# Seven of sixteen heads turned by DMA instead of by TensorE in the first stage of a two-layer gated attention and expert kernel

## The reference, cut to what matters

```python
q = _split_heads(hidden_states_query @ Wq.T + bq)
k = _split_heads(hidden_states_key @ Wk.T + bk)
v = _split_heads(hidden_states_key @ Wv.T + bv)
scale = 1.0 / np.sqrt(HEAD_DIM)
scores = jnp.einsum('bhqd,bhkd->bhqk', q * scale, k)
scores = scores + ((1.0 - attention_mask) * -10000.0)[:, None, :, :]
probs = jax.nn.softmax(scores, axis=-1)
ctx = jnp.einsum('bhqk,bhkd->bhqd', probs, v)
```

## Time and profile before

| | us |
|---|---|
| median of 3 runs | 1444.75 (1437.92 to 1447.92) |
| the profiled execution | 1443.42 |
| its span in the profile | 1441.8 |
| PE busy | 1264.8 (88%) |
| DVE busy | 1092.9 (76%) |
| ACT busy | 1003.9 (70%) |
| POOL busy | 827.7 (57%) |

### The profile page before, as it was taken

How to read it: one execution, slowest core, us unless ns; L and a number is a source line. 1 busy time by engine, 2 the same in 40 slices (tenths; PEclk the granted TensorE clock), 3 DMA queues, 4 the chain that set the end, 5 groups by cost and what they waited for, 6 DMA issues and landing times. The chain is left out here.

```text
span 1441.8 us, 44028 instructions
## 1 busy us (share of the span) xinstructions
PE 1264.8 (88%) x13508; PEld 916.7 (64%) x13508; DVE 1092.9 (76%) x3110; ACT 1003.9 (70%) x2584; POOL 827.7 (57%) x1204
## 2 busy tenths in 40 slices
PE   5999999999985599999998999999999985389994
PEld 3788888888864245656665556656566653278993
DVE  4899999999984268887887877878788873367772
ACT  3988788887883368787776777777787872155662
POOL 3645444454455445777676776777677675045663
PEclk9999999999997699999999999999999996599997
DMA  6233343333400148877666766767576784753323
GB/s 172 86 120 112 106 121 98 118 99 121 120 24 17 48 92 160 159 137 148 136 148 136 151 137 140 141 145 156 122 146 138 146 186 85 285 173 60 61 35 74
DMA packets 303968, 175.19 MB, mean 122 GB/s; under 512 B 250234, under 2 KB 291586, under 8 KB 300720
## 3 DMA queue, kind: packets, MB, share of 16 engines
q1 hardware_dynamic: 287632, 130.94, 40.8%
q0 software_dynamic: 13168, 35.80, 9.8%
q10 hardware_dynamic: 3024, 6.47, 1.6%
HBM read 64.48 MB, written 41.96 MB: 74 GB/s over the span
## 5 line engine op out<-in xcount | busy, mean ns | idle before, releaser
L1663 ACT ACTIVATE b_prob<-b_prob,b_top 112x487 f32<-112x487 f32 x256 | 178.9, 699 | 42.8 <-DVE b_top L1789 40.9
L1296 POOL TENSOR_TENSOR b_halves<-b_prob,b_halves 112x487 f16<-112x487 f32 x128 | 152.3, 1190 | 88.4 <-ACT b_halves L1688 86.6
L1474 PE MATMUL b_ps_p<-w_s,b_tok_s 128*128 128x512 f16 (+1 forms) x768 | 187.7, 381 | 5.6 <-DVE b_k_s L1776 5.3
L1474 PE MATMUL b_ps_p<-b_tok_s,w_s 128*128 128x487 f16 x768 | 188.0, 384 | 4.7 <-POOL b_tok_s L1290 3.7
L1789 DVE CUSTOM_DVE_ANT_0 b_prob<-b_ps_s,b_keep 112x487 f32<-112x487 f32 x256 | 167.7, 656 | 32.1 <-PE b_ps_s L1567 31.8
L701 ACT ACTIVATE a_prob<-a_prob,a_top 112x375 f32<-112x375 f32 x256 | 156.4, 611 | 4.5 <-DVE a_top L837 3.4
L1688 ACT ACTIVATE b_halves<-b_prob 112x487 f16<-112x487 f32 x256 | 156.0, 609 | 0.4
L837 DVE CUSTOM_DVE_ANT_0 a_prob<-a_ps_s,a_keep 112x375 f32<-112x375 f32 x256 | 138.6, 541 | 21.8 <-PE a_ps_s L593 19.2
L1582 PEld LDWEIGHTS b_ps_o<-b_v_s,b_pT 128*128 128x128 f16 (+1 forms) x3072 | 124.9, 100 | 32.7 <-DMA b_pT<-b_halves 11.0
L1582 PE MATMUL b_ps_o<-b_v_s,b_pT 128*128 128x64 f16 (+1 forms) x3072 | 136.1, 195 | 9.0 <-DMA b_pT<-b_halves 8.9
L842 DVE TENSOR_TENSOR a_pT<-a_ps_t,a_pT 125x336 f16<-125x336 f32 x256 | 128.6, 503 | 18.4 <-ACT a_pT L708 12.4
(11 more groups left out here) (262 smaller groups left out, 3063.0 us busy)
## 6 DMA issues: line engine op xcount, KB each, us to landing
xs<-a_blank SPq DMA_DIRECT2D x14, 1032.0 KB, 4.0
c_w_pool<-w_split SPq DMA_DIRECT2D x8, 1600.0 KB, 10.9
b_wch_f<-in_w_experts POOLq DMA_DIRECT2D x32, 384.0 KB, 4.9
w_split<-b_wch_s POOLq DMA_DIRECT2D x32, 384.0 KB, 4.0
a_ctx_f<-in_ctxT SPq DMA_DIRECT2D x16, 375.0 KB, 3.9
a_k_stack<-a_k_s SPq DMA_DIRECT2D x64, 93.8 KB, 2.8
b_ctx_t<-in_ctx SPq DMA_DIRECT2D x16, 375.0 KB
c_xt<-xs SPq DMA_DIRECT2D x35, 129.0 KB, 2.5
```

The lines of the kernel that those rows point to most:

```text
L1296: pool.tensor_tensor(halves[:, h % TURN, LO, 0:NK], prob[:, h % RING, 0:NK], halves[:, h % TURN, HI, 0:NK], ALU.subtract).then_inc(s_lo[1], 1)
L1474: last = pe.matmul(out, sta(a, k), mov(m, k), start=(k == 0 and n == 0), stop=(k == tiles - 1 and n == 2))
L1663: act.activation(prob[:, h % RING, 0:NK], prob[:, h % RING, 0:NK], ACT.Exp, bias=top[:, h % RING:h % RING + 1], scale=-1.0, accum_out=sums ...
```

## The change

Of the 16 heads of each batch of the first stage, seven (`BY_DMA`: 1, 3, 5, 7, 9, 11, 13) no longer go through PE's transposes. ACT copies their exponentials to f16 rows (`high_half`, in slot h+1), POOL makes the low rows (`low_half`, slot h+2), and SP turns both by one transposing DMA (`turn`, slot h+3). Their value products stand six slots behind their scores, those of the nine others (`BY_PE`) four, as before; slot 5 has none and slot 3 of the next batch has two. The nine share one bank `ps_t` (before two). The freed bank holds the second half of the values: heads 0 to 7 are in one bank, 8 to 15 in the other, read out in slots 15 and 4 (of the next batch). Blocks of keys are 128, 128 and 119 (before 3 x 125). `v_s` has a column of ones behind the 32 value columns, so the value product gives the row sums too, and the exponentials are taken without accumulator.

The lists of POOL and SP, before one item after the other, are now given by slot, with the low halves and the turns between the other items. `load_residual` is issued a batch earlier, the store a batch later. `pT` grows from four to eight heads, and POOL sets five more regions at the start, which the other engines wait for. The semaphores of the turns are made once for both stages, so the second stage counts on from what the first has sent.

```diff
-        pT = sb("pT", [128, RING, 2, NB0, 128], F16)
+        TURN = 8
+        prob = sb("prob", [T, RING, CP], F32)
+        halves = sb("halves", [T, TURN // 2, 2, CP], F16)
+        pT = sb("pT", [128, TURN, 2, NA, 128], F16)
...
+        BY_DMA = tuple(range(1, H - 2, 2))
+        BY_PE = tuple(h for h in range(H) if h not in BY_DMA)
+        VSLOT = {s: [s - 4] if s % 2 == 0 else [s - 6] for s in range(4, H + 4)}
+        VSLOT[5] = []
+        VSLOT[H + 3] = [H - 3, H - 1]
@@ SyncE @@
+            def turn(b, h):
+                need_all(sp, settled, (s_lo, len(BY_DMA), b, BY_DMA.index(h) + 1), valued(b, h - TURN))
+                sp.dma_start(pT[:, h % TURN, :, :, 0:T].rearrange("p s j n -> p (s j) n"),
+                             halves[:, h // 2 % (TURN // 2), :, :].rearrange("p s n -> p (s n)"),
+                             transpose=True).then_inc(s_turned[h // 2 % (TURN // 2)], 16)
             def body(b, par):
+                for s in range(H):
+                    if s == 1 and ahead(b, 1):
+                        load_mask(b + 1, 1 - par)
+                    if s == 2 and not early(b, 2):
+                        store(b - 2)
+                    if s == 3 and ahead(b, 2):
+                        load_tokens(b + 2)
+                    if s == 5 and ahead(b, 1):
+                        stack_keys(b + 1, 1 - par)
+                    if s == 9 and ahead(b, 1):
+                        mask_queries(b + 1, 1 - par)
+                    if s == 11:
+                        clear_rows(b)
+                    if s == 13:
+                        load_residual(b)
+                    c, _, h = heads(s, 3, b, par)
+                    if h in BY_DMA and not (first(b) and s < 3):
+                        turn(c, h)
...
 @@ GpSimd @@
             def body(b, par):
+                for s in range(H):
+                    if s == 0 and not first(b):
+                        residual_bias(b - 1)
+                    if s == 1 and ahead(b, 1):
+                        deviation_x(b + 1)
+                    if s == 2 and ahead(b, 1):
+                        mask_bias(b + 1, 1 - par)
+                    if s == 4 and not first(b):
+                        residual(b - 1)
+                    if s - 2 in BY_DMA:
+                        low_half(b, s - 2)
+                    if s == 5 and not first(b):
+                        deviation_x1(b - 1)
+                    if s == 6 and ahead(b, 1):
+                        split_queries(b + 1)
+                    if s == 8 and ahead(b, 2):
+                        context_high(b + 2)
+                    if s == 10 and ahead(b, 2):
+                        context_low(b + 2)
+                    if s >= 12 and not first(b):
+                        add_expert(b - 1, s - 12, ahead(b, 2))
+                    if s >= 8 and first(b):
+                        experts_low(s - 8)
...
             def exps(b, h):              # ACT
+                act.activation(prob[:, h % RING, 0:C], prob[:, h % RING, 0:C], ACT.Exp, bias=top[:, h % RING:h % RING + 1],
+                               scale=-1.0).then_inc(s_exp, 1)
+            def high_half(b, h):
+                act.activation(halves[:, h // 2 % (TURN // 2), HI, 0:C], prob[:, h % RING, 0:C], ACT.Copy).then_inc(s_hi, 1)
@@ TensorE @@
             def values(b, par, h):
+                if h in BY_DMA:
+                    need(pe, *turned(b, h))
+                        last = pe.matmul(ps_o[h // 8][:, col:col + VW - 1], pT[0:r, h % TURN, part, j, :],
+                                         v_s[par][0:r, j, h, 0:VW - 1], start=(h % 8 == 0 and j == 0 and part == HI),
+                                         stop=(j == NA - 1 and part == LO), skip_group_check=True)
@@ VectorE @@
+            def read_out(c, i):
+                dve.reciprocal(rsum[:, group], out[:, :, 2 * D0]).then_inc(s_rsum, 1)
+                dve.tensor_tensor(o_f[:, group, :], out[:, :, 0:D0], o_lo[:, group, :], ALU.add).then_inc(s_oread, 1)
```

More of the change, by code:

```diff
@@ L385, in _ @@
             mask_queries(0, 0)
-            sp.wait_ge(s_blank, 1)
+            sp.wait_ge(s_zero, 2)
             run_batches(sp, body)
+            turn(B - 1, H - 3)
+            store(B - 2)
             store(B - 1)
@@ L455, in next_low, with add_expert, finish @@
                 pool.tensor_tensor(next_w[:, LO, cols], next_f[:, cols], next_w[:, HI, cols], ALU.subtract).then_inc(s_nlo, 1)
[L457 to L465, removed]
+            def add_expert(c, j, alone=True):
+                if not alone:
+                    for n in range(2):
+                        next_low((c - (B - 3)) * 8 + 2 * j + n)
+                need(pool, s_scaled, E // 2, c, j + 1)
+                need(pool, s_odd if j else s_x2, E // 2 if j else 1, c, j)
+                pool.tensor_tensor(acc_odd[:, :], scaled[j % 2][:, :], (acc_odd if j else x1)[:, :], ALU.add).then_inc(s_odd, 1)
+            def finish(c):
                 need(pool, s_odd, E // 2, c, E // 2)
@@ L471, in body @@
             def body(b, par):
-                if ahead(b, 1):
-                    deviation_x(b + 1)
-                if not first(b):
-                    residual(b - 1)
-                    deviation_x1(b - 1)
-                if ahead(b, 1):
-                    mask_bias(b + 1, 1 - par)
-                    split_queries(b + 1)
-                if ahead(b, 2):
-                    split_context(b + 2)
-                if not first(b):
-                    sum_experts(b - 1, ahead(b, 2))
-                if first(b):
-                    for n in range(H // 2):
-                        experts_low(n)
-            split_context(0)
+                for s in range(H):
[21 more added lines that the diff above has]
+                        experts_low(s - 8)
+                if not first(b):
+                    finish(b - 1)
+            context_high(0)
+            context_low(0)
             mask_bias(0, 0)
@@ L619, in values @@
                 last.then_inc(s_pv, 1)
-            def drain(b, par):
-                for s in range(4):
-                    for lag, stage in ((2, transposes), (4, values)):
-                        h = H + s - lag
-                        if h < H:
-                            stage(b, h) if lag == 2 else stage(b, par, h)
             def body(b, par):
@@ L630, in body @@
                     scores(b, par, s)
-                    if not (first(b) and s < 2):
-                        c, _, h = heads(s, 2, b, par)
+                    c, _, h = heads(s, 2, b, par)
+                    if h in BY_PE and not (first(b) and s < 2):
                         transposes(c, h)
-                    if s == 5:
-                        values(b, par, 0)
-                    if s != 4 and not (first(b) and s < 4):
-                        values(*heads(s, 4, b, par))
+                    for h in VSLOT.get(s + H, []):
+                        if not first(b):
+                            values(b - 1, 1 - par, h)
+                    for h in VSLOT.get(s, []):
+                        values(b, par, h)
                     if ahead(b, 1):
@@ L651, in _ @@
             run_batches(pe, body)
-            drain(B - 1, 1)
+            for s in range(H, H + 4):
+                if s - 2 < H:
+                    transposes(B - 1, s - 2)
+                for h in VSLOT[s]:
+                    values(B - 1, 1, h)
             for k in range(DI):
@@ L1114, in phase_attention_large_heads @@
         s_lo = [sem("lo_even"), sem("lo_odd")]
-        s_turned = [sem(f"turned{i}") for i in range(RING)]
         s_pv = sem("pv")
@@ L2273, in build_program @@
         s_rows = ctx.enter_context(nc.semaphore("rows"))
+        s_turned = [ctx.enter_context(nc.semaphore(f"turned{i}")) for i in range(4)]
         with nc.sbuf_tensor("w1_s", [128, 2, WKV + WQ + WOUT], F16) as w1_s:
```

205 lines of the change are left out of this document (120 added, 85 removed).

## The result

The changed kernel takes **1552.88 us** as the median of 4 runs (1550.92 to 1557.06), the kernel before 1446.34 in the same comparison. The ratio is **1.0744**, with a 95% interval of 1.0682 to 1.0806. The direction of the forecast was right, the size was not: 1468 was forecast, 1484 was the top of the range. All runs in this document are in the chip's fast state but one of e10's six, which is left out of its time and ratio.

The account below looks back on a forecast made before the run. PE was taken to set the first stage's pace, DVE close behind. Fourteen batches x 1.1 (15.4), clock 7 and ends 2 gave +24.4 on 1443.4 us: 1468 us, range 1434 to 1484 (without rival outcomes 1454 to 1484).

Parts of the forecast that it names:

- The chain through POOL and SP: First stage: head 7's turn waits on SP behind `mask_queries`, is issued at 13.2 and lands 16.3 us after the read-out.
- When does PE want it?: First stage, slot 13: PE is ready for head 7's values 13.1 us after the read-out.
- the 3 us stall: First stage, slot 13: PE stands about 3 us at head 7's values in each batch that prepares a next one.
- the total of PE's waits for turned heads in the stage: Sign of the forecast: PE's values wait for transposed `a_pT`, 35 to 45 us in total, always behind eight mask transfers.
- The rest of the loop, 10.6 us: First stage, from head 7's values to the next read-out: 11.06 us before, 10.6 after, making the period 26.9 us.
- Rival 3: First stage: POOL's two-input low parts hold up DVE's two normalisations by up to 0.9 us each, 1493 us; chance 0.05.
- The clock: 0.5 us a batch: First stage: half clock behind PE's 3 us stall costs 0 to 1.2 us a batch, taken as 0.5, 7 us over 14 batches.
- The other stages only get other semaphore counts: nothing: Outside the first stage: only semaphore counts change, so no time is added.
- The ends of the stage: First stage, batches 0, 14, 15 and drain: late POOL low parts against a missing stall and a shorter normalisation, sum +2 us.
- The capacity argument: First stage: if only capacity counted, the 25.8 us period would fall to 23.6, or about 23.9 with the second read-out.

Follow-up runs that it names:

- e10: e7 with POOL's low part of head 9 waiting until the gate weights are written: 1463.8 us, ratio 1.0132.
- e4: e1 with `clear_rows` (1 MB to DRAM) moved on SP from slot 11 to slot 15: 1480.5 us, ratio 1.0210.
- e3: e1 with POOL's `context_low` moved from slot 10 to the end of slot 14: 1501.2 us, ratio 1.0356.
- e11: e10 with POOL adding the expert's part ahead of two next-stage low parts in the last two batches: 1455.9 us, ratio 1.0093.
- e1: The changed kernel with 16 more small DVE instructions ahead of its first-stage loop: 1506.6 us, ratio 1.0382.
- e7: e6 with `clear_rows` at slot 1, POOL's `mask_bias` at slot 4 and 40 small ACT instructions ahead of the loop: 1460.1 us, ratio 1.0073.
- e9: e7 without the 16 DVE instructions ahead of the loop, their tile kept: 1515.9 us, ratio 1.0497.
- e6: e1 with `context_low` at slot 14, `clear_rows` at slot 15 and `mask_queries` in halves at slots 9 and 11: 1482.1 us, ratio 1.0199.
- e5: e1 with `mask_queries` split into halves of four copies at slots 9 and 11: 1496.9 us, ratio 1.0347.
- e2: The kernel before with 100 more small DVE instructions ahead of its first-stage loop: 1477.5 us, ratio 1.0178.

## Why the prediction was wrong in size

**The chain through POOL and SP: right, to 0.4 us.** Take the start of the read-out (L953) at 294.15 as zero. Predicted and read: POOL's low part of head 5 ends after 6.7, 6.4; its turn is issued by 8.0, 7.7; `mask_queries` ends at 13.2, 13.0; PE takes up head 7 at 16.3, 15.9. The rows of the zero and of the low part:

```profile
294.15 0.20 DVE L953 RECIPROCAL a_rsum<-a_ps_o 112x8 f32<-112x8 f32 x1
...
299.69 0.90 POOL L468 TENSOR_TENSOR a_halves<-a_prob,a_halves 112x375 f16<-112x375 f32 x1
```

The estimated prices held as well: 1.21 us for the issue of a turn (1.22), 3.0 to its landing (3.1), 0.90 for a low part (0.90):

```profile
L402 SPq DMA_TRANSPOSE a_pT<-a_halves x112: 1202/1212/2103, 33.3 to 539.6; - x112
...
DMA to landing us min/median/max: 2.6/3.0/8.7
```

**"When does PE want it?": wrong by 2.3 us.** I had PE there at 13.1 after the read-out; it came at 15.4 (310.05 - 0.51 - 294.15), of which 1.47 are its wait for the gate weights. So the 3 us stall was 0.5, and the total of PE's waits for turned heads in the stage, 43.6 us where I gave 35 to 45, is right by luck: head 7 has only 12 of it, head 9 has 20, heads 11 and 13 have 8, heads 1 and 3 the rest, and 26 of the 43.6 lie outside 130 to 410 us.

**"The rest of the loop, 10.6 us": wrong by 3.2.** From head 7's values to the next read-out it took 323.87 - 310.05 = 13.8. My step priced DVE's and PE's work there and followed no queue: I stopped at turn 7, though `clear_rows` stands two slots on, and its 1 MB delays the turn of head 9. PE's wait of 2.07 us for that head is most of the 3.2 in this batch; out of the turns' way, `clear_rows` gave back 26 us of the run (e4). I followed the turns behind one transfer of the two that the change puts them behind.

**Rival 3, the collision: right in kind, wrong in place.** I looked for the low parts beside the two normalisations only, found none, and gave it 0.05. The hold falls on the small instructions of the ranking, a 0.17 us cast most visibly, and PE needs their result next; the maxima were not held. Of the Trainium skill's two conditions (GPSIMD Engine Reference, section 1. Specifications) the `cw` sum, which adds two tensors of SBUF, meets the second; for the cast, with one input, only the first can be meant, and no run shows its mode. e3 and e11 show the hold itself; in time neither the 5 us at e1 nor anything at e7 can be told from noise.

**"The clock: 0.5 us a batch".** I had one gap in mind and read from the earlier trace rows that 2.2 us does not lower the clock. After shows a lower clock behind a gap of 2.07 us (313.1 to 315.2) and, at the loop's stop, for longer than the 3.4 us that I priced:

```profile
220.90:227.80 6.90, 3.48 (x19) 2.36 (x20) 3.18 (x10) 1.63 (x4) 1.27 (x3) 0.51 0.02 3
...
316.50:319.90 3.40, 3.40 (x19) 2.16 (x18) 2.01 (x8) 1.80 (x4) 1.66 (x4) 0.50 0.37 97
```

Half clock is 1.2 GHz. Between 130 and 410 us it covers some 41 us, 4.7 per batch. Nearly all of it comes with the stops at the jump: in the same stretch the mean granted clock is 0.93 in after and 0.91 in e9, which have them, but 0.99 in e1 and 1.00 in e3 and e4, which have not, although PE's waits for turned heads in e3 reach 2.7 us. So my term, 0.5 us a batch for a gap at head 7, does not describe what lowered the clock here. What half clock costs alone was not separated from the gaps that bring it.

**"The other stages only get other semaphore counts: nothing".** This is the step with the largest error behind it. An edit also moves all code behind it. DVE's loop lay 7 instructions earlier, and this alone is worth 46 us (e1 against after) to 56 (e9 against e7). By the traces 41 and 46 us of that lie in the first stage; how much the stops of DVE and ACT in the second stage cost is not shown. Without DVE's stop after would have stood at 1507, with `clear_rows` out of the way as well at 1480. That is inside my range, but partly by luck: in e4 PE waits 0.5 to 0.7 us a batch for head 7, not 3, and 1.4 for the gate weights, which I had at nothing. The ends of the stage had +2 in my sum; in e7 they take 12 of the 15 us listed below. The capacity argument was sound: in e7 PE waits 22.1 us in 280, which is 2.0 in a period of 25.8, so its work is 23.7, against 23.6 to 23.9 predicted.

**What stays of the change.** With the causes found removed or made smaller, e7 and e11 run the batch at before's pace, 25.8 and 25.6 us, and still take 0.7 and 0.9% longer. Of e7's 15.1 us of span, 5.0 lie in batches 0 to 4, 1.9 up to batch 15, 5.3 between batch 15's maxima and the second stage, 3.5 in the second stage (within what single traces differ by) and -0.6 behind. What PE saves is paid out again in its waits: per batch 0.8 us for an exponential, 0.6 for `cw`, 0.2 for turned heads, the rest in short ones. The 5 us at the start were not traced.

## What to carry to other kernels

Before an edit to a kernel with loops is judged, compare the count of code packets on the page and look for stops with "issue" at the jump: here seven instructions fewer ahead of a loop of 303 brought the stop, and 16 idle ones took it away. When a latency-bound step is put on a shared queue, list everything that queue and the DMA engines carry up to the last use, not up to the first, and name the head that a wait is for by its slot before a cure is chosen (e6). And a wait of the bound engine that is taken away only pays if the next thing in line is ready: in e3, e5 and e11 it moved on instead.

## What the hardware showed that was not expected

- A jump back to code that, by the packets, is loaded again stops VectorE for 2.9 to 3.1 (e2), 6.4 to 7.6 (after) or 8.5 to 8.6 us (e9), once per turn of the loop. Five packets are loaded per turn in all three, but one of them starts within the stop in e2 and two do in after and e9. Why e9's stop is longer than after's stays open; the DMA engines are 0.80 busy in e2's stop and 0.79 in e9's.
- A GpSimd instruction with two inputs holds a small VectorE instruction of the ranking until it ends: 0.17 us become 1.23 or 0.82, and the ends agree to 0.03 us. The maxima beside the same work keep their 0.54 us.
- A 1 MB transfer between two turns makes the next one's issue 2.01 us long instead of 1.21, and its landing 5.0 us instead of the 2.6 of the turn of head 3 (medians of batches 5 to 12 of after).
